# A banded local-attention stage: scores in 64x32 and values in 64x64 TensorE tiles, one copy for q and probabilities, new orders

## What is computed

```
q, k, v = split(shift(x) @ Wqkv)            # 16 heads of 64, windows of 32 tokens
q, k    = rotary(l2norm(q)*qs)*scale, rotary(l2norm(k)*ks)/scale
sim     = 8 * q_window @ [k_previous_window, k_window].T    # 32 queries x 64 keys
sim     = where(key > query or key < query - 32 or no window, -max, sim)
x       = x + (softmax(sim) @ [v_previous_window, v_window]) @ Wo
a, gate = split(layernorm(shift(x)) @ W1 + b1)              # 2 x 341
x       = x + (a * gelu(gate)) @ W2 + b2
```

## Time and profile before

| | |
|---|---|
| median of 3 runs | 2273.87 us |
| lowest, highest | 2270.52, 2282.59 us |
| span of the profiled execution, first to last instruction | 2279.7 us |
| mean granted TensorE clock | 0.944 of full |
| PE, PEld busy | 88%, 59% of the span |
| DVE, ACT, POOL busy | 80%, 73%, 56% of the span |

### The profile page before, as it was taken

One profiled execution on the slowest core, in us unless ns is written; L12 is line 12 of the kernel. 1 busy time (PEld: TensorE's weight loads), 2 busy tenths in 40 slices (PEclk: granted clock), 3 DMA queues, 4 the chain that ended last, 5 costly groups with the idle time before them and its releaser, 6 DMA issues. The chain is left out here.

```text
span 2279.7 us, 55457 instructions
## 1 busy us (share of the span) xinstructions
PE 2005.6 (88%) x20349; PEld 1350.3 (59%) x20349; DVE 1815.6 (80%) x3618; ACT 1660.3 (73%) x3144; POOL 1267.3 (56%) x1132
## 2 busy tenths in 40 slices
PE   5788888689999999999999999999999999985274
PEld 3333333356766776776676767677667767764153
DVE  4666663699999999999999999999999999944633
ACT  2255556378888888888888888888888888874123
POOL 4400000577677777767767766776776776731052
PEclk8699998799999999999999999999999999997587
DMA  6311100111111121111211112111211111100512
GB/s 159 101 42 44 23 2 11 58 36 38 30 39 29 35 82 29 39 29 39 78 29 39 30 41 75 31 37 30 87 30 29 39 30 38 30 29 26 188 34 68
DMA packets 70562, 107.36 MB, mean 47 GB/s; under 512 B 20887, under 2 KB 47774, under 8 KB 68734
## 3 DMA queue, kind: packets, MB, share of 16 engines
q1 hardware_dynamic: 68262, 100.87, 15.4%
q0 software_dynamic: 1280, 2.62, 0.4%
q10 hardware_dynamic: 752, 0.33, 0.1%
HBM read 41.60 MB, written 12.26 MB: 24 GB/s over the span
## 5 line engine op out<-in xcount | busy, mean ns | idle before, releaser
L1583 POOL TENSOR_TENSOR qk<-rot_cos,rot_sin 128x512 f32<-128x512 f32 x256 | 323.2, 1273 | 154.6 <-DVE rot_sin L1361 154.6
L1593 POOL TENSOR_TENSOR qk<-qk,rnorm 128x512 f32<-128x512 f32 x256 | 263.1, 1043 | 88.0 <-DVE rnorm L1394 88.0
L1359 DVE TENSOR_TENSOR rot_cos<-pA,layer_tab 128x512 f32<-128x512 f32 x384 | 263.2, 685 | 60.1 <-ACT sq L1171 55.1
L434 ACT ACTIVATE probs_by_key<-pT 128x512 f32<-128x512 f32 (+3 forms) x384 | 177.1, 490 | 155.4 <-PE pT L320 121.0
L499 DVE TENSOR_REDUCE minus_max<-pS 128x1 f32<-128x1024 f32 (+7 forms) x256 | 184.6, 754 | 110.0 <-PE pS L290 109.2
L1171 ACT ACTIVATE sq<-pA 128x512 f32<-128x512 f32 x384 | 228.5, 595 | 53.1 <-PE pA L890 43.6
L1371 DVE TENSOR_REDUCE sumsq<-sq 128x8 f32<-128x512 f32 x384 | 253.6, 671 | 14.3 <-ACT sq L1171 14.2
L1361 DVE TENSOR_TENSOR rot_sin<-pA,layer_tab 128x512 f32<-128x512 f32 x384 | 261.1, 680 | 0.0
L1231 ACT ACTIVATE probsT<-pD 64x512 f32<-64x512 f32 x380 | 224.0, 589 | 35.3 <-PE pD L931 31.9
L1600 POOL TENSOR_TENSOR probs<-probs,row_inverse 128x1024 f32<-128x1024 f32 x96 | 182.6, 1903 | 100.3 <-DVE row_inverse L1430 100.3
L1191 ACT ACTIVATE qT<-pC 64x512 f32<-64x512 f32 x384 | 225.9, 588 | 7.3 <-PE pC L905 0.5
(11 more groups left out here) (342 smaller groups left out, 4659.0 us busy)
## 6 DMA issues: line engine op xcount, KB each, us to landing
v_shifted<-v SPq DMA_DIRECT2D x96, 384.0 KB, 3.5
v_shifted<-v SPq DMA_DIRECT2D x95, 128.0 KB, 3.4
q_stack<-stacked SPq DMA_DIRECT2D x24, 192.0 KB
k_stack<-stacked SPq DMA_DIRECT2D x24, 192.0 KB
W_ahead<-in_Wqkv_dram SPq DMA_DIRECT2D x12, 384.0 KB
layer_weights<-in_Wqkv_dram SPq DMA_DIRECT2D x12, 384.0 KB
stacked<-part SPq DMA_DIRECT2D x32, 128.0 KB, 2.4
tokens_in<-tokens SPq DMA_DIRECT2D x2, 1024.0 KB
```

The costliest lines, as they stand in the source:

```text
L1359: dve.tensor_tensor(t1[c % 2][:, :].rearrange("p (h g d) -> p h g d", g=2, d=32), a, tabl[s % 2][:, j].unsqueeze(1).broadcast_to([P, 8, 2, ...
L1583: pool.tensor_tensor(qk(s, c), t1[c % 2][:, :], t2[c % 2][:, :], ALU.add).then_inc(added[c], 1)
L1593: pool.tensor_tensor(v, v, rn[p % 2][:, o:o + 8].unsqueeze(2).broadcast_to([P, 8, DH]), ALU.mult).then_inc(scaled[c], 1)
```

## The change

It touches only `window_layers`.

1. `S` takes a whole tile: 64 matmuls of 64 rows x 32 columns of weights (one head, one window of 32 queries) against 64 keys. Head b of a pair uses the lower or upper 64 rows of the array and writes to bank C[b]; the four 32-row strips of the bank hold the windows. The innermost loops go through eight array tiles before one comes again.
2. `PV` takes a whole tile: 64 matmuls of 64 rows (the window pair wp) x 64 columns (one head's values) against 32 columns of probabilities, bank Db[wp], four array tiles in turn.
3. qT and PTz lose the zero halves (from 2048 to 1024 columns), and `qt` and `pev` are one instruction each. A memset on DVE and one on POOL at the start go.
4. `s_ready` and `o_ready` are one semaphore each, so `S` waits for both halves of q and of the mask, and `PV` for both halves of the probabilities. `oev` copies the same number of elements, cut by window pair.
5. All orders are rewritten, the loop runs PAIRS + 1 times and not PAIRS + 2, and the drain is written out at length. `x2` of a pair now comes in round r = pair + 6 and not pair + 5. The drain uses the ordinary banks.

```diff
-        qT = sb("qT", [P, 8, 4, 2, 32])
+        qT = sb("qT", [P, 8, P])
-        PTz = sb("probsT", [P, 8, 4, 2, 32])
+        PTz = sb("probsT", [P, 8, P])
...
-            def S(u, p, k):
+            def S(p, k):
                 s = tile(p, k)
-                pe.wait_ge(q_kept[u], s + 1)
-                pe.wait_ge(masked[u], s + 1)
-                for hp in range(4):
-                    for wi in range(4):
-                        j, wp = wi % 2, wi // 2
-                        o = s % 2 * P + 32 * wi
-                        mm = pe.matmul(C[u][64 * j:64 * j + 64, hp * P + 64 * wp:hp * P + 64 * wp + 64],
-                                       qT[:, 4 * u + hp, wi, :, :], KT[:, 4 * u + hp, o:o + 64],
-                                       start=False, stop=True, skip_group_check=True)
-                mm.then_inc(s_ready[u], 1)
+                for u in range(2):
+                    pe.wait_ge(q_kept[u], s + 1)
+                    pe.wait_ge(masked[u], s + 1)
+                for a in range(4):
+                    for wp in range(2):
+                        for z in range(2):
+                            for j in range(2):
+                                for b in range(2):
+                                    hp, row = 2 * a + z, slice(64 * b, 64 * b + 64)
+                                    q, o = 64 * wp + 32 * j, k * P + 64 * wp + 32 * j
+                                    mm = pe.matmul(C[b][64 * j + 32 * z:64 * j + 32 * z + 32, a * P + 64 * wp:a * P + 64 * wp + 64],
+                                                   qT[row, hp, q:q + 32], KT[row, hp, o:o + 64],
+                                                   start=False, stop=True, skip_group_check=True)
+                mm.then_inc(s_ready, 1)
...
-            def PV(u, p, k):
+            def PV(p, k):
-                pe.wait_ge(pt_kept[u], s + 1)
+                for u in range(2):
+                    pe.wait_ge(pt_kept[u], s + 1)
                 pe.wait_ge(v_shifted[s % 3], shifts(s))
-                for hp in range(4):
-                    out = probs_bank(u, p, k)[:, hp * P:(hp + 1) * P].rearrange("p (w j q) -> p j w q", w=2, j=2)
-                    for j in range(2):
-                        for b in range(2):
-                            h = 8 * u + 2 * hp + b
-                            mm = pe.matmul(out[64 * b:64 * b + 64, j], (Vs, Vn)[j][s % 3][:, h * DH:(h + 1) * DH],
-                                           PTz[:, 4 * u + hp, 2 * j + b, :, :], start=True, stop=True, skip_group_check=True)
-                mm.then_inc(o_ready[u], 1)
+                for a in range(4):
+                    for z in range(2):
+                        for j in range(2):
+                            for b in range(2):
+                                for wp in range(2):
+                                    h, c = 4 * a + 2 * z + b, (2 * a + z) * 64 + 32 * j
+                                    row = slice(64 * wp, 64 * wp + 64)
+                                    mm = pe.matmul(Db[wp][64 * b:64 * b + 64, c:c + 32], (Vs, Vn)[j][s % 3][row, h * DH:(h + 1) * DH],
+                                                   PTz[row, 4 * b + a, 64 * j + 32 * z:64 * j + 32 * z + 32],
+                                                   start=True, stop=True, skip_group_check=True)
+                mm.then_inc(o_ready, 1)
...
-                for b in range(2):
-                    rows = slice(64 * b, 64 * b + 64)
-                    a = act.activation(qT[rows, 4 * u:4 * u + 4, :, b, :],
-                                       C[u][rows, :].rearrange("p (h w q) -> p h w q", h=4, w=4), AF.Copy)
-                a.then_inc(q_kept[u], 1)
+                act.activation(qT[:, 4 * u:4 * u + 4, :], C[u][:, :].rearrange("p (h q) -> p h q", h=4), AF.Copy).then_inc(q_kept[u], 1)
...
-            for r in range(PAIRS + 2):
+            for r in range(PAIRS + 1):
```

More of the change, by code:

```diff
@@ new lines, in drain @@
+                kt(0, LAST, 0)
+                mk(0, LAST, 0)
+                pev(1, LAST - 2, 1)
+                ex(1, LAST - 1, 1)
+                ex(0, LAST - 1, 1)
+                vev(0, LAST, 0)
+                xnT(LAST - 3)
+                vev(1, LAST, 0)
+                qt(0, LAST, 1)
+                oev(1, LAST - 2, 1)
+                kt(0, LAST, 1)
+                oev(0, LAST - 2, 1)
+                qt(1, LAST, 1)
+                ex(1, LAST, 0)
+                ex(0, LAST, 0)
@@ new lines, in drain @@
+                mk(0, LAST, 1)
+                ge_(LAST - 3)
+                kt(1, LAST, 1)
+                mk(1, LAST, 1)
+                pev(0, LAST - 1, 0)
+                pev(1, LAST - 1, 0)
+                vev(0, LAST, 1)
+                oev(0, LAST - 1, 0)
+                vev(1, LAST, 1)
+                oev(1, LAST - 1, 0)
+                pev(0, LAST - 1, 1)
+                pev(1, LAST - 1, 1)
+                ex(1, LAST, 1)
+                ex(0, LAST, 1)
+                xnT(LAST - 2)
@@ new lines, in drain @@
+                oev(1, LAST - 1, 1)
+                oev(0, LAST - 1, 1)
+                ge_(LAST - 2)
+                pev(0, LAST, 0)
+                pev(1, LAST, 0)
+                oev(0, LAST, 0)
+                oev(1, LAST, 0)
+                pev(0, LAST, 1)
+                pev(1, LAST, 1)
+                xnT(LAST - 1)
+                oev(1, LAST, 1)
+                oev(0, LAST, 1)
+                ge_(LAST - 1)
+                xnT(LAST)
+                ge_(LAST)
+            if r == PAIRS:
@@ new lines, in dve_body @@
+            ss(3, r - 1, 0)
+            x2(r - 6)
+            sub(1, r - 2, 0)
+            rot(0, r - 1, 1)
+            ss(1, r - 1, 1)
+            sum_(r - 3, 1)
+            ss(0, r - 1, 1)
+            rec(r - 3, 1)
+            rot(1, r - 1, 1)
+            rot(2, r - 1, 1)
+            ya(r - 4)
+            ss(2, r - 1, 1)
+            ss(3, r - 1, 1)
+            nw(r - 1)
+            rot(3, r - 1, 1)
+            mx(0, r - 2, 1)
+            mx(1, r - 2, 1)
+            sub(0, r - 2, 1)
@@ L1516, in dve_body @@
+            sub(1, r - 2, 1)
             ga(r - 5)
```

603 lines of the change are left out of this document (336 added, 267 removed).

## The result

The changed kernel took **2480.57 us** (median of 4 runs, 2466.75 to 2482.01) against 2272.19 for the kernel before (median of four runs, 2270.23 to 2282.59; the 2273.87 above is that of three of them): a ratio of **1.0889, 95% interval 1.085 to 1.0927**. It is slower by 8.9%, where I had forecast 2224 us and a gain.

A forecast was written before the change was run, and what follows sets the result against it. PE was taken as the bound with 1.3 us of slack a round, DVE next. Span 2279.7 - 55 (1.2 us a round over 46 rounds) + 5 (ends) = 2229.7, less 5.8: 2224 us, range 2175 to 2345.

The forecast's parts named there:

- Scores after: Scores on PE: 128 records over eight array tiles at 13.5 ns each, 1.73 us a tile, -0.3 us a round.
- Values after: Values on PE: 128 records on four array tiles at 14.6 ns each, 1.87 us a tile, no change.
- Rival 3: Long PE streams: fixed time per record whatever its size, twice the records; 2431 us at 23 ns, 2357 at 20; chance 0.14.
- Rival 4: Scores and values: the array's two row halves don't overlap, +5.1 us a round less 1.0 of slack, 2468 us; chance 0.11.
- The change of shape: PE switching tile shapes: three visits a round become two with a change inside each, 1.16 against 1.02 us, +0.1 a round.
- The orders' term: PE's new order: `W2`'s wait of 1.11 us a round for DVE's `ga` goes, as other work covers it.
- Late next is DVE itself: After the new orders, DVE is what comes late next, at 31.8 us of a round, against PE's 31.9.
- The ends: Start and drain: one loop turn less, `x2` half a round later, longer drain; +5 us, between -15 and +17.
- 3.8 us of cover less 3.0: PE's work between last key transposes and `S`, 3.8 us, covers ACT's five copies, 3.0 us, with 0.6 to spare.
- rival 2: No change: values pay start steps on top (+1.3 us a round) or a new order waits elsewhere; 2270 us, chance 0.12.
- a round stays near 31.8: DVE as next bound: whatever PE gains, a round stays near 31.8 us, so the middle gives 75 us at most.
- The copies: ACT's `qt` and `pev`: half of the instructions go, 4.7 us a round off ACT, 29.0 to 24.4, worth nothing by itself.

The follow-up runs named there:

- e4: Changed kernel plus three streams of 512 matmuls behind PE's drain (64x32, 64x64, 128x64 tiles): 2563.57 us, one run; streams 30.17, 28.8 and 30.8 us.
- e7: Changed kernel plus four streams of 64x32 tiles behind PE's drain, 512, 256, 128 and 64 columns: 2559.64 us, one run; 53.7, 27.0, 27.7, 28.3 ns a pair.
- e5: e2 with each tile's scores in two halves, a V between them, and Wa or V ahead of the values: 2605.06 us, ratio 1.1413.
- e6: Changed kernel with each tile's scores in two halves, a V between them, and Wa or V ahead of the values: 2555.09 us, ratio 1.1212.
- e1: Changed kernel with its new orders, but scores and values in the old 128x64 tiles with zero padding and two copies each: 2298.83 us, ratio 1.0077.
- e3: Changed kernel with scores back in the old padded 128x64 tiles and values in the new 64x64 tiles: 2328.87 us, ratio 1.0218.
- e2: Changed kernel with scores in the new 64x32 tiles and values back in the old padded 128x64 tiles: 2326.10 us, ratio 1.0214.

## Why the prediction was wrong

**The step that failed** is the pair "Scores after" and "Values after". Both priced a record by how fast the array can start it, from bursts of eight records. Both array figures held or were cautious: 128 scores in 1.41 us where I took 1.73, values at 14.6 ns as taken. But the sum had no term for getting the instructions to the engine. e4 and e7 give it: 28 to 30 ns a pair in a long run, 3.5 to 4.0 us for 128 pairs. The 256 pairs more of a round are two pieces more. No row of before shows the limit by itself: its runs at 29.2 ns need a piece every 3.74 us, just what the supply gives, so that any faster pair had to hit it. What the prediction did have is its own remark that no row shows a long stream below 29.2 ns; it gave that 0.14 and took the burst for the rule.

**Rival 3 had the right side and the wrong form.** It put a fixed time on each record of a long stream, 20 to 29 ns. The records really go at 9.9 and 14.6 ns, and the time is taken once per piece and only where a piece is worked off too fast. So its place depends on what stands beside the stream, which is why e5 and e6 could remove the waits with the same count of records. Its 2357 to 2431 us stayed under the 2480.57 measured, because of two things that it lacks. First, a piece's transfer can be late: of 114 waits of over 0.9 us, 110 have their packet begun 0.07 to 1.3 us ahead of them. In the other four, with 3.0 to 5.4 us, it begins 0.6 to 2.8 us after PE has stopped, and there the DMA engines are busy, 0.33 to 0.59 of each wait (at 1467.18 with the next layer's weights); in all the others but one (2.3 us long, 0.64) they are busy for under 0.05. Secondly the clock: 184 us at half of full take up to 92 us more (an estimate: no more than half of them).

By the figure of the Trainium skill's TensorEngine Tiling (Array Packing), Instruction Overhead, some 25 ns a matmul (an estimate from its 60 cycles), a round came out near rival 3's middle. A long stream is close to that (27.7 to 30), but not for its reason: between waits the records of the kernel after follow each other at 9.9 ns, so there is no such overhead for each matmul here.

Rival 4 (row halves don't overlap) named nearly the right time, 2468 us, but by luck, for a reason that e7 excludes. A record of 512 columns alone takes 0.86 / 2 = 0.43 us, and eight at once would be 430 / 8 = 53.8 ns each; e7 measured 53.7, so all eight tiles, both row halves among them, overlap fully.

**The account by parts.** The scores gain 2 x (1.87 - 1.41) = 0.9 us a round, more than the 0.3 taken. The values gain 0, as taken. The change of shape was not told apart. The waits are 221 us over 46 rounds, 4.8 a round. The slack of the round takes a part of them and the low clock adds to them; no run tells the two apart. Together it is +3.8 a round. The orders' term, -1.1 a round for `W2`'s wait, was right about that wait (it appears in no kernel with the new orders) and wrong about its worth, since e1 has another of the same size and rounds of 33.4 us. "Late next is DVE itself" was wrong: in e1 and e3, which keep its two copies, late next was ACT's `qT`; with one copy no such wait shows. The ends cost +18.9 where I took +5 (my bound was +17); in e1, whose last part has no supply waits to speak of, +8.5. Three small sums are off and move nothing: 3.8 us of cover less 3.0 are 0.8 and not 0.6, 46 x 1.6 are 74 and not 75, and rival 2's round of 33.4 us makes 2277 and not 2270 us.

**A second reading that failed**, though it did not decide the sign: DVE as the next bound, so that "a round stays near 31.8". In that figure is Newton's first step with 1.92 us, and the same instruction takes 0.23 us in every kernel with the new orders. Before the change each of its 48 runs falls together with an instruction of POOL, 45 of them with this one:
```profile
L1600 POOL TENSOR_TENSOR probs<-probs,row_inverse 128x1024 f32<-128x1024 f32 x96 | 182.6, 1903 | 100.3 <-DVE row_inverse L1430 100.3
```
The step ends 0.08 us after POOL's instruction all 48 times; in the first three places that is an `add` (L1583), which is shorter, and there the step takes 1.19 to 1.28 us. In the new orders POOL does nothing in any of the 48 places, and DVE's work falls from 31.0 to 29.0 us a round (e1) and 29.1 (the kernel after). That POOL holds the step up is argued from this coincidence; no run moved it alone. So the room for a gain was larger than the prediction had it: of the 3 us a round by which DVE waits longer behind `sq` in e1 than before, 2 can be this room.

**The copies** behaved as forecast: `qT` is one instruction of 0.605 us over 128 partitions, and ACT's work fell from 29.1 to 23.9 us a round (forecast 24.4). What that is worth by itself no run shows.
```profile
L1229 ACT ACTIVATE qT<-pC 128x512 f32<-128x512 f32 x34 | 19.7, 605 | 0.2 <-PE pC L891 0.2
```

**What stays open.** How much of the 3.8 us a round is the low clock alone (no run held it full with the waits in place); whether the weight transfers cause the four long waits or only coincide with them, since no run moved them away; whether POOL alone makes Newton's first step long; and whether an order exists that gets e2's 31.3 us in every round.

## What to carry to other kernels

Count instructions as a resource with a rate of its own: here TensorE got 128 pairs of weight load and matmul per 3.5 to 4.0 us, so a run of pairs shorter than about 28 ns gains nothing beyond the first one or two hundred. Before splitting matmuls into smaller tiles, look at the `instruction` queue on the page and at gaps whose releaser is `issue`, and ask whether 128 consecutive pairs anywhere take less than some 3.6 us. If they do, mix them with long matmuls whose inputs are long ready, and check on each engine what the moved piece was covering. Here that won back most of the loss (8.9% to 0.9%) and did not make a gain of it. And before a busy engine is called the next bound, look whether one of its instructions takes longer than its equals of the same shape: that time can go with the order.

## What the runs showed of the hardware that I had not expected

- Instructions of TensorE come in pieces of 16.4 KB, and each 128 pairs of a fast stream end in a stop of 1.1 to 2.3 us (e4, e7), at full clock as at a lower one. Only one piece seems to be fetched ahead. Advanced Engine Details and Errata of the Trainium skill, section ISA Cache, gives TensorE 128 KB and in the same list two lines of 16 KB. The runs side with two lines: a store of eight pieces, filled ahead, would have carried the 256 pairs of a visit after some 9 us of long matmuls (1458.33 to 1467.18 us), and they stopped all the same.
- Eight 64x32 tiles run at once: pairs of 64 columns start every 9.9 ns within a piece, and pairs of 512 every 53.7 ns, where one alone takes 430.
- Newton's first step on DVE takes 0.23 us by itself and 1.9 us where POOL's `norm` of 1.9 us had begun just before it: it ended 0.08 us after POOL's instruction in all 48 places of the kernel before.
- A wait of PE of 5.15 us was followed by 4.83 us at half clock (1.2 GHz), in which the values took 1.5 us longer than in the good place; e5 had 246 us of that level from waits for another engine.
